# Layer 0 of a four-layer triangle-multiplication kernel: its result held in SBUF, channel sums on TensorE, and the entry's loads and first weight fold moved

## The reference

```python
x = x + conv(group_norm(x), parameters)          # four times
def conv(x):
    xn = layernorm(x)                             # over the 64 channels
    left, right = (xn @ Wl) * sigmoid(xn @ Wlg), (xn @ Wr) * sigmoid(xn @ Wrg)   # masked in layers 0, 2
    out = einsum('bikh,bjkh->bijh', left, right)  # per channel, a 256x256x256 product
    return (layernorm(out) * sigmoid(xn @ Wog)) @ Wo
```

## Time and profile before

| what | value |
|---|---|
| median of three runs | 2247.53 us |
| the profiled execution's own time | 2251.78 us |
| its span, first to last instruction | 2250.0 us |
| busy: TensorE / VectorE / ScalarE / GpSimd | 1980.0 / 1752.7 / 1703.8 / 626.9 us |
| entry, x's 16 chunks | 21.0 to 104.2 us |
| layer 0: contract | 312.5 to 361.2 us |
| layer 0: project, half 1 | 361.2 to 429.6 us |
| layer 0: contract_kept | 429.6 to 478.6 us |
| layer 0: finish | 478.6 to 617.3 us |

### The profile page before, as it was taken

The page is one execution under the profiler, slowest core; times in us unless marked ns, Lnnn a source line. Parts: engine busy times, 40 slices in busy tenths (PEclk is TensorE's granted clock), DMA queues, the critical chain, the costliest instruction groups (busy, mean ns, idle before and its releaser), DMA issues. The chain is left out here.

```text
span 2250.0 us, 46969 instructions
## 1 busy us (share of the span) xinstructions
PE 1980.0 (88%) x13892; PEld 1409.8 (63%) x13892; DVE 1752.7 (78%) x2978; ACT 1703.8 (76%) x2741; POOL 626.9 (28%) x590
## 2 busy tenths in 40 slices
PE   4599877869989798998989899899998989899998
PEld 3433767735533697975543397897553359798665
DVE  5668899988858886888958897887775889787665
ACT  2388787869978775967988785676997878595676
POOL 0000555526410000006520081461872000000655
PEclk8699998969999999999999999999999999999999
DMA  8879948469979846647969992945997985673798
GB/s 324 330 218 278 275 127 232 121 228 376 356 217 280 290 161 209 202 173 279 417 256 279 268 278 75 262 113 206 375 419 213 280 286 165 213 236 122 275 346 305
DMA packets 450421, 566.26 MB, mean 252 GB/s; under 512 B 15216, under 2 KB 346992, under 8 KB 433904
## 3 DMA queue, kind: packets, MB, share of 16 engines
q1 hardware_dynamic: 447984, 547.89, 73.4%
q10 hardware_dynamic: 2304, 16.78, 1.8%
HBM read 384.25 MB, written 180.36 MB: 251 GB/s over the span
## 5 line engine op out<-in xcount | busy, mean ns | idle before, releaser
L765 PE MATMUL bank<-whigh,kept 128*128 128x128 f16 x4096 | 507.3, 227 | 66.4 <-DMA kept<-XH 31.0
L765 PEld LDWEIGHTS bank<-whigh,kept 128*128 128x128 f16 x4096 | 466.6, 125 | 76.1 <-issue 61.7
L765 PE MATMUL bank<-wlow,kept 128*128 128x128 f16 x4096 | 506.5, 227 | 2.4 <-issue 2.4
L765 PEld LDWEIGHTS bank<-wlow,kept 128*128 128x128 f16 x4096 | 467.1, 125 | 0.0
L1360 POOL TENSOR_TENSOR LR<-LR 128x512 f32<-128x512 f32 x128 | 186.8, 1478 | 529.0 <-DVE LR L1406 506.3
L787 ACT ACTIVATE sigs<-bank,small 128x256 f32<-128x256 f32 x512 | 237.9, 476 | 66.2 <-PE bank L765 59.2
L1351 POOL TENSOR_TENSOR LR<-LR,sum 128x2048 f32<-128x2048 f32 x30 | 136.6, 4552 | 522.3 <-DVE LR L1172 522.3
L630 PE MATMUL bank<-LR,cen 128*128 128x512 f32 x512 | 256.9, 627 | 22.7 <-DMA LR<-XT 11.5
L686 DVE SCALAR_TENSOR_TENSOR LR<-bank,small,LR 126x1024 f32<-126x1024 f32 x128 | 164.3, 1284 | 121.8 <-ACT LR L663 121.4
L787 ACT ACTIVATE squares<-bank,small 128x256 f32<-128x256 f32 x512 | 237.3, 476 | 14.6 <-PE bank L765 6.3
L638 PE MATMUL bank<-LR,kst 128*128 128x512 f32 x512 | 240.9, 593 | 5.2 <-ACT LR L659 5.2
(11 more groups left out here) (150 smaller groups left out, 3639.7 us busy)
## 6 DMA issues: line engine op xcount, KB each, us to landing
LR<-XT SPq DMA_DIRECT2D x128, 512.0 KB, 5.2
kept<-XH SPq DMA_DIRECT2D x128, 512.0 KB, 6.3
LR<-XT SPq DMA_DIRECT2D x64, 1024.0 KB, 9.6
kept<-XHA SPq DMA_DIRECT2D x128, 512.0 KB, 4.6
XT<-LR SPq DMA_DIRECT2D x48, 1024.0 KB, 9.1
LR<-XH SPq DMA_DIRECT2D x64, 512.0 KB, 7.2
LR<-XHA SPq DMA_DIRECT2D x64, 512.0 KB, 6.2
OS<-kept SPq DMA_DIRECT2D x12, 2048.0 KB, 7.7
```

The source lines that it names most:

```text
L765: last = pe.matmul(bank(g)[:, j * P:(j + 1) * P], tokens, w[:, half * P:(half + 1) * P], start=part == 0, stop=part == 1)
```

## The change

Four parts.

First, the entry. SP's first instructions are the first four loads of x; constants, parameters and mask are loaded at the same time on ScalarE's DMA queue, and nobody waits for them until TensorE's first transpose and VectorE's fold. The block of the fold is gone: its pieces stand between the chunks of the entry, whose loops are written out. The entry uses six PSUM banks for transposes where it used eight, since the fold uses banks 6 and 7.

Second, layer 0's contraction. One function, `contract_low`, takes the place of `contract` and `contract_kept` in layer 0, for both halves. The result of half 0 stays in SBUF (LR's slots 8 to 11) instead of going to OSL and back, that of half 1 in `kept0`. ScalarE copies the even steps out of PSUM, VectorE the odd ones. The sum over channels is made by TensorE: a matmul of a bfloat16 identity with the result, accumulated over eight steps in one PSUM bank, which VectorE takes once for each of the two row tiles. VectorE still adds the squares.

Third, what follows from it: `project` half 1 finds its first four XH chunks loaded during the contraction, its TensorE waits for the sums to be taken, and `finish` in layer 0 has no OSL loads, and three XH buffers instead of four.

Fourth, both halves of `contract_low` load ScalarE's table for logarithm and exponential; `project` is unchanged and asks for the sigmoid table in half 0 alone.

```diff
+        with nc.Block() as block:
             @block.sync
             def _(sp):
                 for h in range(4):
                     load_x(sp, h)
+                for s in sems:
+                    sp.sem_inc(s.s, CREDIT)
             @block.scalar
             def _(act):
-                fold_act(act)
+                act.dma_start(kst[:, :], consts).then_inc(prep.s, 16)
+                load_parameters(act, 0)
...
+                pe.wait_ge(prep.s, prep.n + 48)
+                for t in range(4 * NCH):
+                    turn(t)
+                    if t == 10:
+                        fold_project(pe)
+                    if t == 20:
+                        fold_turn(pe)
+                    if t == 28:
+                        fold_spread(pe)
...
+                unrolled(4 * NCH, (pair, 0), (count, 4), (prepare_weights, 0))
...
-                for h in range(2, 4):
+                for h in range(4 if half == 1 and layer["low"] else 2, 4):
                     load_xh_chunk(sp, h, h, k_is_b)
...
                     pe.wait_ge(copied.s, copied.n)
+                    pe.wait_ge(copied_v.s, copied_v.n)
+                    pe.wait_ge(sums_taken.s, sums_taken.n)
...
-                    nrm, xh, xt = (11, 12, 7), (13, 0, 1, 2), (14, 15, 3, 6)
+                    self.os = None
+                    nrm, xh, xt = (12, 2, 7), (13, 0, 1), (14, 15, 3, 6)
...
+        def contract_low(block, number, layer, half):
...
+            @block.tensor
+            def _(pe):
+                def sum_channels(e):
+                    ut, g = parts[e]
+                    if e % 2 == 0:
+                        pe.wait_ge(copied.s, copied.n + e // 2 + 1)
+                    else:
+                        pe.wait_ge(copied_v.s, copied_v.n + e // 2 + 1)
+                    for two in range(2):
+                        last = pe.matmul(by_channels(bank(4 + ut)), ident_low[:, :], result(e)[:, 2 * two:2 * two + 2, :],
+                                         start=(g, two) == (0, 0), stop=(g, two) == (7, 1))
+                    last.then_inc(channel_sums.s, 1)
...
+                    for c in range(4):
+                        for kt in range(NT):
+                            last = pe.matmul(banks[e % 2][:, c * N:(c + 1) * N],
+                                             LRb[:, kt, 4 * g + c, ut * P:(ut + 1) * P],
+                                             LRb[:, kt, HALF + 4 * g + c, :], start=kt == 0, stop=kt == NT - 1)
+                    last.then_inc(contracted.s, 1)
+                    if e >= 1:
+                        sum_channels(e - 1)
+                sum_channels(15)
+            @block.scalar
+            def _(act):
+                act.preload_act_table_set("natural_log_exp_and_others")
...
+                    if e % 2 == 0:
+                        act.wait_ge(contracted.s, contracted.n + e + 1)
+                        act.activation(result(e), by_channels(banks[0][:, :]), ACT.Copy).then_inc(copied.s, 1)
+                        act.wait_ge(copied.s, copied.n + e // 2 + 1)
+                    else:
+                        act.wait_ge(copied_v.s, copied_v.n + e // 2 + 1)
+                    if e >= 2:
+                        act.wait_ge(summed.s, summed.n + 2 * (e - 1))
+                    act.activation(by_channels(squares[e % 2][:, :]), result(e), ACT.Square).then_inc(squares_ready.s, 1)
+            @block.vector
+            def _(dve):
+                def copy(e):
+                    dve.wait_ge(contracted.s, contracted.n + e + 1)
+                    dve.tensor_copy(result(e), by_channels(banks[1][:, :])).then_inc(copied_v.s, 1)
...
+                    for two in range(2):
+                        if e or two:
+                            dve.wait_ge(summed.s, summed.n + 2 * e + two)
+                        dve.tensor_tensor(sum2[:, ut, :], sum2[:, ut, :],
+                                          squares[e % 2][:, 2 * two * N:2 * (two + 1) * N],
+                                          ALU.add).then_inc(summed.s, 1)
+                def take_sums(ut):
+                    dve.wait_ge(channel_sums.s, channel_sums.n + 8 * ut + 8)
...
+            @block.sync
+            def _(sp):
+                if half == 0:
+                    load_parameters(sp, number + 1)
+                    sp.wait_ge(contracted.s, contracted.n + 1)
+                    for h in range(4):
+                        load_xh_chunk(sp, h, h, layer["k_is_b"])
```

## The result

The changed kernel takes 2221.98 us (median of four runs, 2219.76 to 2222.64) against 2247.07 us: 25.1 us less, a ratio of 0.9882 with an interval of 0.9865 to 0.9899. The forecast was 2229.6 us, 17.9 less, in a range of 2219 to 2241. It is faster, as forecast, and 7.6 us faster than its likeliest case, just outside that case's own 2223 to 2236.

The account below looks back on a forecast made before the run. The prediction took bytes to bound the entry, VectorE the contractions, ScalarE the finish. Terms -8.3 - 6.7 + 3.1 - 6.0 = -17.9 us, from the 2247.5 us median, gave 2229.6 us, range 2219 to 2241.

Parts of the forecast that it names:

- The entry, -8.3: Entry: loads 9.2 us earlier, 1.9 us of DMA idleness gone, constants sharing the stream +2.8; -8.3 us in sum.
- the hole: Entry: DMA engines stand still between the first four loads and the next ones; removing this saves 1.9 us.
- Contraction of half 0, -6.7: Layer 0's first contraction: VectorE loses half its adds but gains copies; 42.0 us against 48.7, -6.7.
- the 1.7 us added for TensorE: Contraction of half 0: allowance of 1.7 us for TensorE's part of the fold and half-clock stretches.
- Contraction of half 1, -6.0: Layer 0's second contraction: same VectorE list plus moments and first chunk's normalization; 43.0 us against 49.0, -6.0.
- Project half 1, +3.1: Project half 1: later start with chunks already there -1.2, four sigmoid table loads +4.3; +3.1 us in sum.
- the handoff: Start of project half 1: XH chunks already there, but TensorE waits for VectorE's last take; -1.2 us.
- Finish, 0: Layer 0's finish: no OSL loads and three XH buffers instead of four cost 0, between -2 and +2 us.
- The half clock: Both contractions: TensorE stays at half clock and replaces VectorE as bound; -1.2 us in all, 2246 us; 10%.
- The drain: Project half 1: each table load also drains the engine, 10.6 us instead of 4.3; kernel 2236 us; 8%.
- the starved finish: Layer 0's finish: three XH buffers starve it; at 25 us per load the kernel takes 2279 us; 4%.
- The third: Entry, contractions, project half 1: cheap copies, entry not byte-paced, free reloads; mixture -24 to -28, about 2221 us; 8%.

Follow-up runs that it names:

- e3: The changed kernel with ScalarE making 12 of each layer 0 contraction's 16 PSUM copies, VectorE steps 3, 7, 11 and 15; 2220.33 us, ratio 0.9861.
- e8: The kernel before with only the entry's four loops over chunks written out; 2247.07 us against 2250.3 in the same round, ratio 0.9984.
- e2: The changed kernel with four store buffers instead of two for the entry's transposed chunks; 2218.73 us, ratio 0.9877.
- e5: The changed kernel with x's loads still first, but the fold in one piece ahead of the first chunk; 2234.47 us, ratio 0.9945.
- after: The first profile of the changed kernel itself, with nothing further altered; span 2220.2 us.
- e6: The changed kernel with the fold still spread, but x's loads issued behind the constants; 2231.93 us, ratio 0.9922.
- e1: The changed kernel with sigmoid's table loaded once ahead of layer 0's project half 1, not in each round; 2221.64 us, ratio 0.9879.
- e9: The changed kernel with two XH buffers instead of three in layer 0's finish; 2223.49 us (one run).
- e10: The changed kernel with each channel-sum matmul issued twice in layer 0's contractions; 2220.70 us (one run).

## Why the prediction was right, and where it was off

**The bound.** Right in the main: the contractions were VectorE's and shrank with its list. No run separates the channel sums on TensorE from the result kept in SBUF, so -10.1 and -6.3 belong to both together; and e3 shows that a shorter list doesn't always shorten the stage by as much. That bytes set the entry is half the matter. With two store buffers the copies of each of the last 14 chunks start 0.02 us behind the landing of a store, so a lag in that chain counts (e8) although the DMA share is 1.0; with four buffers bytes bound it (e2).

**The entry, -8.3.** What was priced, early loads and no hole against the constants in the stream, measures -9.1 (e8 to the changed kernel). The split was wrong: the prediction has -9.2 and +2.8 for loads and constants even if the hole stays, and e5 shows that early loads alone give nothing. And one part of the change has no term at all: the loops on four engines are written out. In the loop the chain of stores lagged, and the saturated stretch moved 399 GB/s (29 to 93 us) where the changed kernel moves 413. That gave another 3.4 to 4.3 at the entry's end, 12.7 in the first pair of profiles, beyond the term's own end of -11.5. (That end was added up wrongly too: 0.8 us, 1.5 to the first data and 2.17 MB at 395 GB/s make 7.8 us for the first interleaving, not 9.5; it came at 8.26.) Up to 3 us are waited for again in norm and project half 0, and 10.9 us of the entry's part stay. Since e8 gives back all of its gain there, it stays open what the 2.6 us more than forecast are due to.

**Contraction of half 0, -6.7.** Measured -10.1 (49.1 to 39.0), the term furthest off. VectorE's list was sized well (40.3 for 39.0, with the copy's 1.14 us from start to start for my 1.2). What failed is the 1.7 us added for TensorE: they were not needed where its first products ran at full clock (seven profiles; 0.91 over the stage in after), and e5 and e6 with a slower start took 0.6 more. The copy takes 1.22 us, and the lower end of 0.7 is out. That agrees with what the Trainium skill (VectorE: DVE Perf Modes, "Why PSUM operands drop a tier") says, that float32 from PSUM gets no more than the single rate.

**Contraction of half 1, -6.0.** Measured 42.1 and 42.4 for 43.0: -6.3 between the means.

**Project half 1, +3.1.** Measured +2.2, with two errors that cancel, which is luck. The reloads cost 2.2 and not 4.3 (e1): the first, which I had exposed whole, costs 0.1, and the others 0.6 to 0.7 each for my 1.0. My step took VectorE as the pace that ScalarE must follow chunk by chunk; over four chunks ScalarE has enough to spare to make up half of a load. The other error is the handoff, TensorE's later start with its chunks already there. It saved nothing where I had -1.2 (68.8 us without reloads against 68.3 and 69.2): the first chunk took 8.1 us for my 7.2, at a clock of 0.57, and a chunk 4.05 for my 4.0. The estimate of 10.6 us came from the price of a switch to another set in the Trainium skill (ScalarE: Activation LUTs, "What ACT_TABLE_LOAD costs"), a load of 1283 ns and a drain of about 1380 ns, taken four times. The trace agrees with the load (1.28 us in each row) and shows no drain: the next activation starts 0.02 us behind it.

**Finish, 0.** Measured -0.9 between the means, and e9 shows that even two XH buffers cover the loads.

**The rivals.** The half clock (2246) did not come: 0.91 and 0.92 over the two stages. The drain is out by e1, the starved finish by e9. The third, 2221 by cheap ends, has the right number for the wrong reason (and its sum takes -10 and -9 where its cheap ends are -12.4 and -10): copies were not cheap and reloads not free, while the sum was off by 2.6 us in the entry, 3.4 and 0.3 in the contractions, 0.9 in project half 1 and 0.9 in the finish, all to the same side.

## What to carry to other kernels

List every edit in a diff, the form of its loops too: written-out loops were worth 3.4 to 4.3 us at the entry's end, twice the hole in the stream, and had no term. Loads issued earlier gain only as far as their buffers reach, so move what holds the first buffer together with them. And taking work from the engine that bounds a stage helps only where its order then lets the next engine run: with the same number of copies left to VectorE, four, the adds of half 1 took 34.7 us in one order and 32.7 in another.

## What the runs showed that I had not expected

- A stage's gain can vanish a stage later: in e8's profile the entry was shorter by 3.4 to 4.3 us, and project half 0 ended at 312.5 us all the same, though the kernel's time fell by 0.05 to 0.27%.
- Layers 1 to 3, whose instructions no variant touches, took between 1623.0 and 1628.9 us in fourteen profiles; where these 5.9 us come from stays open.
- TensorE's first 16 matmuls of contract half 0 took 1.92 us in the changed kernel and 3.35 and 3.36 in e10 and e3 (2.4 and 1.2 GHz), and 2.57 and 2.33 in e5 and e6, behind the same 2.8 us of idleness. What decides between them stays open.
